# Causal masks written into the score banks by VectorE and ScalarE instead of by TensorE

## The chip, the core and the metric

The kernel runs on one core of a Trainium2 chip. The metric is the device time of the whole program in microseconds, as the median of several executions. A core has five engines with in-order queues of their own: TensorE (PE in the profile, with its weight loads as PEld), VectorE (DVE), ScalarE (ACT), GpSimd (POOL) and SyncE (SP). They wait for one another through semaphores only. TensorE writes its products to PSUM, which has eight banks of 128 partitions x 512 fp32 values, here named by their use.

## The reference, cut to what matters

Two decoder layers over x of shape (8, 128, 256): each has self attention, cross attention on a context of 64 columns, and an expert block; after each comes a residual sum and a layer norm. Three of the four attentions are causal:

```python
# layer 0 self attention (16 heads of 16)
scores = jnp.einsum('bqhd,bkhd->bhqk', Q, K)
scores = jnp.where(causal[None, None], scores, -jnp.inf)
attn = jax.nn.softmax(scores, axis=-1)
# layer 0 cross attention (32 heads of 8): no mask
# layer 1 self attention (32 heads of 8, rotary): causal
# layer 1 cross attention (16 heads of 16): causal as well
```

## The kernel before, in words

The four attentions run in one stage, the function `attention`, as a list of 32 units: 8 batch rows of ATTN0 (units 0 to 7), of CROSS0 (8 to 15), of ATTN1 (16 to 23) and of CROSS1 (24 to 31). ATTN0, ATTN1 and CROSS1 are causal. A unit has 2 pairs of banks of work if its heads are wide (ATTN0, CROSS1) and 4 if they are narrow (CROSS0, ATTN1), 96 pairs in all, 64 of them causal. The loop goes over places w and steps c of a place (2 or 4 steps). Between CROSS0 and ATTN1 four places host layer 0's expert block, whose products use the S^T banks and PV. All queues are written out by this one loop, so that the order on each engine is fixed by the code.

Softmax needs each row's maximum along q, and the sum with the values needs P transposed. So scores are made twice. S (queries on partitions) goes to two banks SB[0], SB[1], where VectorE takes maxima over each head (L730, in `maxima`). S^T (keys on partitions) goes to STB[0], STB[1]; small products (L356, `subtract_max`) take the maxima off, ScalarE takes exp into pt (L590, in `exponentials`), and `values` (L428) multiplies pt with the values into bank PV.

One step of TensorE is: `fill`, which writes the S pair of a later unit and the S^T pair of the present one together (L336 for S, L344 or L348 for S^T, L356 for the maxima), then `values` of the pair before, then other small jobs of neighbouring units. In a narrow place step c = 0 has the projection (L279), c = 1 the transposes of PV and of q and k (L437, L322) and then `values`, c = 2 the output projection (L447, L455, with ScalarE's copy atT, L608, between), c = 3 the transpose of the maxima (L407; copied back by ScalarE as nm, L602) and of x (L262). A wide place puts the same into two steps: c = 0 has the projections, `values`, the value projection (L302 or L304) and L437; c = 1 has `values`, L407, L262, L447 and L455.

VectorE's queue in a step begins with `maxima` and goes on with what the place needs: norm (L797), rope (L675 to L683), the query and key copies (L690, L707, L712, L699), `normalise` (L761, L768: reciprocal and att, for which `values` at c = 1 waits), `residual` (L782 to L791). ScalarE's begins with `exponentials` and goes on with copies out of PSUM: qT (L562), pvs (L596), vaug (L579), nm, xT (L549), atT.

In a causal unit, `fill` starts each bank with a mask product: an identity of bf16 times a 128 x 512 bf16 mask (0, or -1e30 where masked), with start=True (L372 for SB, L384 for STB). The scores are then added onto it. `fill` waits for max_done (bank SB read) before the S mask products, and for exp_done (STB read) before the S^T ones; at a unit's first S^T pair also for nm_copied.

Of the kernel before, what the change touches and what calls it, by code (L numbers as in the profile page):

```python
# [21 lines left out]
ACT = mybir.ActivationFunctionType  # L22
# [68 lines left out]
class Stage:  # L91
# [5 lines left out]
    def sem(self, name):  # L97
        self.sems.append(self.nc.alloc_semaphore(f"{self.prefix}_{name}"))
        return self.sems[-1]
# [10 lines left out]
def attention(nc, cfgs, T, F):  # L110

    V = B * len(cfgs)
    FFN_AT, FFN_HOSTS = 2 * B, B // 2
    STEPS = 11
    own = [cfgs[v // B] for v in range(V)]
    n = [cfg.pairs for cfg in own]
    before = [sum(n[:v]) for v in range(V + 1)]
# [18 lines left out]
    def emptied(t, q):  # L136
# [2 lines left out]
            return 2 * (q - 1)  # L139
        return 2 * (4 * t + q - 2)  # L140

    def tile_of(w, c):

        return 2 * (w - FFN_AT) + c // 2 if FFN_AT <= w < FFN_AT + FFN_HOSTS else None
# [12 lines left out]
    with Stage(nc, "at") as stage, ExitStack() as ctx:  # L157
        sem = stage.sem
# [12 lines left out]
        v_ones = sem("v_ones")  # L171
        s_done = sem("s_done")
        max_done = sem("max_done")
        nm_hi = sem("nm_hi")
        nm_split = sem("nm_split")
        nmt_done = sem("nmt_done")
# [2 lines left out]
        exp_done = sem("exp_done")  # L179
# [34 lines left out]
        SB, STB = T.SB, T.STB  # L214

        def s_pair(w, c):

            nxt, soon = unit(w + 1), unit(w + 2)
            if c == hosted(w) - 1 and has(soon):
                return soon, 0  # L220
            if has(nxt) and c + 1 < n[nxt]:
                return nxt, c + 1
            return None

        def t_pair(w, c):
            v = unit(w)
            return (v, c) if has(v) and c < n[v] else None
# [21 lines left out]
        def _(pe):  # L249
# [75 lines left out]
            def scores(v, c, u, r):  # L325

                j = 2 * (c % 2) + u
                rows = slice(32 * j, 32 * j + 32)
                first = r == 0 and not own[v].causal
                bank = SB[u][:, r * 256:(r + 1) * 256]  # L330
                if own[v].wide:
                    q, k = T.qT[v % 3][rows, r * 128:(r + 1) * 128], T.kk[v % 3][rows, r * 256:(r + 1) * 256]
                else:
                    g = 2 * (c // 2) + r
                    q, k = T.qT[v % 3][rows, g * 128:(g + 1) * 128], T.kk[v % 3][rows, 0:256]
                return pe.matmul(bank, q, k, start=first, stop=r == 1, skip_group_check=True)  # L336

            def scores_t(v, c, u, r, e):

                j = 2 * (c % 2) + u  # L340
                rows = slice(32 * j, 32 * j + 32)
                if own[v].wide:
                    at = 2 * r + e
                    pe.matmul(STB[u][:, at * 128:(at + 1) * 128], T.kk[v % 3][rows, at * 128:(at + 1) * 128],  # L344
                              T.qT[v % 3][rows, r * 128:(r + 1) * 128], start=(at == 0 and not own[v].causal), stop=False, skip_group_check=True)
                elif r == 0 and e == 0:
                    kind = c // 2
                    pe.matmul(STB[u][:, :], T.kk[v % 3][rows, kind * 128:(kind + 1) * 128], T.qT[v % 3][rows, :],  # L348
                              start=not own[v].causal, stop=False, skip_group_check=True)
# [9 lines left out]
            def fill(w, c):  # L359

                s, t = s_pair(w, c), t_pair(w, c)
                if s:
                    v, i = s
                    p = before[v] + i
                    if i == 0:
                        pe.wait_ge(q_ready, v + 1)
                        pe.wait_ge(k_ready, v + 1)
                    for u in range(2):
                        if p > 0:
                            pe.wait_ge(max_done, 2 * (p - 1) + u + 1)  # L370
                        if own[v].causal:
                            pe.matmul(SB[u][:, :], T.ident_bf[:], T.mask_qk[:], start=True, stop=False, skip_group_check=True)  # L372
                if t:
                    v, i = t
                    p = before[v] + i
                    if i == 0:
                        pe.wait_ge(nm_copied, v + 1)
                        if v == FFN_AT:
                            pe.wait_ge(added, B * E0)
                    for u in range(2):  # L380
                        if p > 0:
                            pe.wait_ge(exp_done, 2 * (p - 1) + u + 1)
                        if own[v].causal:
                            pe.matmul(STB[u][:, :], T.ident_bf[:], T.mask_kq[:], start=True, stop=False, skip_group_check=True)  # L384
                for r in range(2):
                    if s:
                        for u in range(2):
                            last = scores(*s, u, r)
                            if r == 1:
                                last.then_inc(s_done, 1)  # L390
                    if t:
                        for e in range(2):
                            for u in range(2):
                                scores_t(*t, u, r, e)
                if t:
                    for slot in range(4):
                        for u in range(2):
                            last = subtract_max(*t, u, slot)
                            if slot == 3:
                                last.then_inc(st_done, 1)  # L400
# [108 lines left out]

            for w, c, count in hosts:  # L510
                fill(w, c)
                if count == 2 and c == 0:
                    project(unit(w + 2))
# [30 lines left out]
        def _(act):  # L544
# [36 lines left out]
            def exponentials(pair):  # L581
                if not pair:
                    return
                v, c = pair
                t = before[v] + c
                if t >= 2:
                    act.wait_ge(pv_done, t - 1)
                for u in range(2):
                    act.wait_ge(st_done, 2 * t + u + 1)
                    act.activation(T.pt[2 * (t % 2) + u][:, :], STB[u][:, :], ACT.Exp, scale=own[v].scale).then_inc(exp_done, 1)  # L590

            def copy_pv(m):
                if not has(m):
# [69 lines left out]
        def _(dve):  # L663
# [59 lines left out]
            def maxima(pair):  # L723
                if not pair:
                    return
                v, c = pair
                for u in range(2):
                    dve.wait_ge(s_done, 2 * (before[v] + c) + u + 1)
                    at = 4 * (c // 2)
                    dve.tensor_reduce(T.nmf[v % 2][:, 2 * (c % 2) + u, at:at + 4], SB[u][:, :].rearrange("p (h k) -> p h k", h=4),  # L730
                                      AX.X, ALU.max, negate=True).then_inc(max_done, 1)

            def split_maxima(m):
                if not has(m):
# [1121 lines left out]
```

## Time and profile before

| | us |
|---|---|
| median of 3 runs (lowest, highest) | 892.03 (890.66, 892.32) |
| the profiled execution, its own time | 893.14 |
| its span, first to last instruction | 891.2 |

| engine | busy us | share of the span |
|---|---|---|
| PE | 741.9 | 83% |
| PEld | 457.1 | 51% |
| DVE | 473.9 | 53% |
| ACT | 294.9 | 33% |
| POOL | 209.2 | 23% |

The mean granted TensorE clock was 0.952. The attention stage runs from about 40 to 572 us, the expert block of layer 0 from about 250 to 343 us within it; the rest up to 891 us is the routing and the experts of layer 1. Shares of busy time average over these stages, and a busy TensorE in this view is not one at its peak, since the ends of pipelined matmuls are modelled. A timeline row gives the start, the duration, the engine, the line and the tiles of a run of like instructions, and in brackets how long the engine sat idle before it and what ended that.

### The profile page before, as it was taken

To read this page: it belongs to the slowest core of one execution; us is meant where nothing else is said; L and a number is where in the kernel's file an instruction comes from. 1 tells how busy PE (TensorE), PEld (TensorE's weight loads), DVE (VectorE), ACT (ScalarE), POOL (GpSimd) and SP (SyncE) were. 2 spreads that over 40 slices of the span, in tenths; PEclk is the share of its full clock that TensorE was granted. 3 is DMA by queue.
4 is the path that set the end of the run, shared out by engine and by line. 5 is a ranking of instruction groups with operands and counts; after the bars stand their busy time and mean duration, and the time that the engine had idled before them with its cause. 6 is when DMAs were issued, how large, how long until landed. Compare 5 with 4: busy or idle time off the path is not lost. (4 is left out here: it accounts for less than half of the span.)

```text
span 891.2 us, 18175 instructions
## 1 busy us (share of the span) xinstructions
PE 741.9 (83%) x6832; PEld 457.1 (51%) x6887; DVE 473.9 (53%) x1240; ACT 294.9 (33%) x702; POOL 209.2 (23%) x253
## 2 busy tenths in 40 slices
PE   3589987877799999999999998699699999999900
PEld 3457765555554455655566666467344433434400
DVE  5755565566448886455453454259533333333447
ACT  0013233444420102333333333233265544555400
POOL 3111222010000000000000000054456556665500
PEclk9999999999969999999999999879899999999955
DMA  9493002000000000000000000087122222222273
GB/s 295 122 293 110 2 3 95 1 3 1 2 1 1 0 1 1 1 1 2 2 1 2 1 3 1 1 224 214 32 75 84 78 84 80 82 84 78 73 244 103
DMA packets 48123, 55.28 MB, mean 62 GB/s; under 512 B 7366, under 2 KB 43174, under 8 KB 47334
## 3 DMA queue, kind: packets, MB, share of 16 engines
q1 hardware_dynamic: 38246, 34.11, 13.2%
q0 software_dynamic: 6656, 16.85, 5.6%
q10 hardware_dynamic: 3136, 3.15, 1.1%
q8 instruction: 58, 0.95, 0.5%
q14 instruction: 27, 0.22, 0.1%
HBM read 41.45 MB, written 12.65 MB: 61 GB/s over the span
## 5 line engine op out<-in xcount | busy, mean ns | idle before, releaser
L730 DVE TENSOR_REDUCE nmf<-bank 128x4 f32<-128x512 f32 x192 | 123.7, 686 | 123.6 <-PE bank L336 123.5
L590 ACT ACTIVATE pt<-bank 128x512 f32<-128x512 f32 x192 | 104.2, 595 | 252.8 <-PE bank L356 252.8
L336 PE MATMUL bank<-kk,qT 32*128 32x256 f32 x768 | 109.2, 401 | 15.9 <-ACT pt L590 8.3
L928 POOL TENSOR_TENSOR rstd<-vare,half 128x1 f32<-128x1 f32 x32 | 17.5, 546 | 376.9 <-DVE vare L791 376.9
L336 PEld LDWEIGHTS bank<-kk,qT 32*128 32x128 f32 x768 | 67.2, 184 | 51.2 <-issue 35.3
L1531 PE MATMUL bank<-wgu,g_xgT 128*64 x256 | 90.5, 476 | 2.1 <-ACT g_xgT L1568 1.2
L1531 PE MATMUL bank<-g_wgu,g_xgT 128*64 128x352 f32 x256 | 90.5, 476 | 0.0
L356 PE MATMUL bank<-nm,sel 32*128 32x128 f32 x768 | 84.5, 338 | 0.0
L1496 POOL DMA_INDIRECT out_rows<-g_og,g_out_row x64 | 63.9, 998 | 64.9 <-DVE g_og L1600 54.5
L348 PE MATMUL bank<-qT,kk 32*128 32x512 f32 x256 | 74.6, 659 | 2.0 <-ACT pt L590 1.5
L1551 PE MATMUL bank<-wd,g_hT 128*64 x256 | 68.9, 392 | 0.2
L1551 PE MATMUL bank<-g_wd,g_hT 128*64 128x256 f32 x256 | 69.0, 392 | 0.0
L1491 POOL DMA_INDIRECT g_xg<-x_rows,g_x_row x64 | 62.6, 978 | 23.0 <-issue 18.2
L356 PEld LDWEIGHTS bank<-nm,sel 32*128 32x128 f32 x768 | 57.4, 191 | 18.1 <-issue 18.1
L1600 DVE COPY g_og<-bank 128x256 f32<-128x256 f32 x64 | 27.0, 421 | 65.9 <-remote 52.6
L491 PE MATMUL bank<-f_m,f_xT 128*128 128x512 f32 x128 | 59.6, 605 | 0.6 <-DVE f_acc L837 0.5
L1582 ACT ACTIVATE g_wgu<-wgu 128x704 f32 x64 | 50.7, 792 | 14.5 <-issue 9.1
L428 PE MATMUL bank<-pt,vaug 128*32 128x128 f32 x1024 | 43.0, 287 | 10.3 <-DVE att L768 9.6
L1594 DVE TENSOR_TENSOR g_h<-bank,g_sil 128x176 f32<-128x176 f32 x64 | 21.7, 339 | 55.9 <-ACT g_sil L1572 43.6
L1531 PEld LDWEIGHTS bank<-wgu,g_xgT 128*64 128x64 f32 x256 | 30.1, 137 | 33.2 <-issue 31.3
L1551 PEld LDWEIGHTS bank<-wd,g_hT 128*64 128x64 f32 x256 | 29.8, 136 | 21.7 <-issue 12.5
L1568 ACT ACTIVATE g_xgT<-bank 128x256 f32<-128x256 f32 x64 | 24.1, 377 | 40.0 <-remote 29.4
(242 smaller groups left out, 1346.5 us busy)
## 6 DMA issues: line engine op xcount, KB each, us to landing
wgu<-in_L_ffn_w_gate SPq DMA_DIRECT2D x4, 1408.0 KB
wgu<-in_L_ffn_w_up SPq DMA_DIRECT2D x4, 1408.0 KB
wd<-in_L_ffn_w_down SPq DMA_DIRECT2D x32, 176.0 KB
g_y<-out_rows SPq DMA_DIRECT2D x4, 768.0 KB, 16.7
g_y<-out_rows ACTq DMA_DIRECT2D x4, 768.0 KB, 17.4
sparse_table<-f_m_re SPq DMA_DIRECT2D x2, 1024.0 KB
f_m_re<-sparse_table SPq DMA_DIRECT2D x2, 1024.0 KB, 5.9
f_idx_row<-in_L_ffn_mask_idx SPq DMA_DIRECT2D x1, 1024.0 KB
```

What stands on the lines that cost most here:

```text
L336: return pe.matmul(bank, q, k, start=first, stop=r == 1, skip_group_check=True)
L348: pe.matmul(STB[u][:, :], T.kk[v % 3][rows, kind * 128:(kind + 1) * 128], T.qT[v % 3][rows, :], start=not own[v].causal, stop=False, skip_ ...
L356: return pe.matmul(STB[u][:, slot * 128:(slot + 1) * 128], T.sel[rows, which, :], T.nm1[rows, :], start=False, stop=slot == 3, skip_group_ ...
L428: last = pe.matmul(PV[quarter * COL:(quarter + 1) * COL, at * 128:(at + 1) * 128], cfg.stationary(vaug(v), kv), T.pt[2 * (t % 2) + u][:, s ...
L491: last = pe.matmul(expert_bank(t, q)[:, :], F.xT[t % 2][:, j * 128:(j + 1) * 128], F.m[:, j, 2 * q:2 * q + 2, :], start=(j == 0), stop=(j ...
L590: act.activation(T.pt[2 * (t % 2) + u][:, :], STB[u][:, :], ACT.Exp, scale=own[v].scale).then_inc(exp_done, 1)
L730: dve.tensor_reduce(T.nmf[v % 2][:, 2 * (c % 2) + u, at:at + 4], SB[u][:, :].rearrange("p (h k) -> p h k", h=4), AX.X, ALU.max, negate=Tru ...
L1491: pool.indirect_dma_start(G.xg[n % 4][:], None, G.x_rows[:, :], bass.IndirectOffsetOnAxis(ap=G.x_row[:, n:n + 1], axis=0)).then_inc(gather ...
L1496: pool.indirect_dma_start(G.out_rows[:, :], bass.IndirectOffsetOnAxis(ap=G.out_row[:, n:n + 1], axis=0), G.og[n % 4][:], None).then_inc(sc ...
L1531: last = pe.matmul(gu[n % 2][rows, 0:2 * MI], G.xgT[n % 2][:, j * 128:(j + 1) * 128][:, rows], w, start=(j == 0), stop=(j == KT - 1), skip ...
L1551: last = pe.matmul(down_bank[n % 2][rows, 0:D], G.hT[n % 2][:, j * 128:(j + 1) * 128][:, rows], w, start=(j == 0), stop=(j == 1), skip_gro ...
L1582: act.activation(G.wgu[n % 2][:], T.wgu[:, bass.ds(unit, 1), :, :].rearrange("p a k n -> p (a k) n"), ACT.Copy).then_inc(wgu_ready, 1)
```

## The change

The masks are now in memory as before, but they are copied into the PSUM banks: VectorE copies mask_qk into SB[u] right behind the pair's two maxima, and ScalarE copies mask_kq into STB[u] right behind the pair's two exponentials. `fill` waits for these copies (s_masked, st_masked) where it waited for max_done and exp_done, and begins with the scores, added onto what lies in the bank. The very first pair has no pair before it, and the first S^T pair of ATTN1 follows the expert block in these banks; these keep mask products. 63 of 64 S pairs and 62 of 64 S^T pairs change over.

```diff
+    pair_units = [v for v in range(V) for _ in range(n[v])]
+    s_masks = [p for p in range(1, len(pair_units)) if own[pair_units[p]].causal]
+    st_masks = [p for p in s_masks if p != before[FFN_AT]]
...
                     for u in range(2):
-                        if p > 0:
+                        if p in s_masks:
+                            pe.wait_ge(s_masked, 2 * s_masks.index(p) + u + 1)
+                        elif p > 0:
                             pe.wait_ge(max_done, 2 * (p - 1) + u + 1)
-                        if own[v].causal:
+                        else:
                             pe.matmul(SB[u][:, :], T.ident_bf[:], T.mask_qk[:], start=True, stop=False, skip_group_check=True)
...
                     for u in range(2):
-                        if p > 0:
+                        if p in st_masks:
+                            pe.wait_ge(st_masked, 2 * st_masks.index(p) + u + 1)
+                        elif p > 0:
                             pe.wait_ge(exp_done, 2 * (p - 1) + u + 1)
-                        if own[v].causal:
+                        if own[v].causal and p not in st_masks:
                             pe.matmul(STB[u][:, :], T.ident_bf[:], T.mask_kq[:], start=True, stop=False, skip_group_check=True)
...
                     act.activation(T.pt[2 * (t % 2) + u][:, :], STB[u][:, :], ACT.Exp, scale=own[v].scale).then_inc(exp_done, 1)
+                if t + 1 in st_masks:
+                    for u in range(2):
+                        act.wait_ge(exp_done, 2 * t + u + 1)
+                        act.activation(STB[u][:, :], T.mask_kq[:], ACT.Copy).then_inc(st_masked, 1)
...
                                       AX.X, ALU.max, negate=True).then_inc(max_done, 1)
+                p = before[v] + c
+                if p + 1 in s_masks:
+                    for u in range(2):
+                        dve.wait_ge(max_done, 2 * p + u + 1)
+                        dve.tensor_copy(SB[u][:, :], T.mask_qk[:]).then_inc(s_masked, 1)
```

VectorE's queue in a place of ATTN1, steps c = 0 and c = 1, before (bank0 and bank1 are SB, bank4 is PV, bank5 and bank6 hold projections; line numbers are those of each kernel):

```order
L730 TENSOR_REDUCE nmf0_153<-bank0 128x4 [waits at_s_done]
L730 TENSOR_REDUCE nmf0_153<-bank1 128x4 [waits at_s_done]
L797 TENSOR_SCALAR x_all_51<-res_179,mv_65,rstd_62 128x256 [waits at_rstd_done]
L675 TENSOR_TENSOR rope_a_183<-bank5,rope_131 128x320 [waits m_cleared]
L678 TENSOR_TENSOR rope_b_184<-bank5,rope_131 128x40x4 x2
L683 TENSOR_TENSOR qs1_163<-rope_a_183,rope_b_184 128x20x16 [waits m_pe,m_act,at_rope_a]
L730 TENSOR_REDUCE nmf0_153<-bank0 128x4 [waits at_s_done]
L730 TENSOR_REDUCE nmf0_153<-bank1 128x4 [waits at_s_done]
L761 RECIPROCAL rec_178<-bank4 128x32 [waits at_pvt_done]
L768 TENSOR_TENSOR att_176<-bank4,rec_178 128x16x2x8 [waits at_at_done,at_rec_done]
```

The same place in the changed kernel, from the first of these steps up to att:

```order
L744 TENSOR_REDUCE nmf0_153<-bank1 128x4 [waits at_s_done]
L750 CAST bank0<-mask_qk_136 128x512 [waits at_max_done]
L750 CAST bank1<-mask_qk_136 128x512 [waits at_max_done]
L816 TENSOR_SCALAR x_all_51<-res_179,mv_65,rstd_62 128x256 [waits at_rstd_done]
L689 TENSOR_TENSOR rope_a_183<-bank5,rope_131 128x320 [waits m_cleared]
L692 TENSOR_TENSOR rope_b_184<-bank5,rope_131 128x40x4 x2
L697 TENSOR_TENSOR qs1_163<-rope_a_183,rope_b_184 128x20x16 [waits m_pe,m_act,at_rope_a]
L744 TENSOR_REDUCE nmf0_153<-bank0 128x4 [waits at_s_done]
L744 TENSOR_REDUCE nmf0_153<-bank1 128x4 [waits at_s_done]
L750 CAST bank0<-mask_qk_136 128x512 [waits at_max_done]
L750 CAST bank1<-mask_qk_136 128x512 [waits at_max_done]
L780 RECIPROCAL rec_178<-bank4 128x32 [waits at_pvt_done]
```

Two copies now stand between the maxima and rope, and two between the maxima and the reciprocal.

ScalarE's queue in a place of ATTN1, steps c = 2 and c = 3, before (bank2 and bank3 are STB, bank7 holds the transposed att):

```order
L590 ACTIVATE pt0_164<-bank2 128x512 [waits at_st_done,at_pv_done]
L590 ACTIVATE pt1_165<-bank3 128x512 [waits at_st_done]
L608 ACTIVATE atT_177<-bank7 128x256 [waits at_at_done]
L590 ACTIVATE pt2_166<-bank2 128x512 [waits at_st_done,at_pv_done]
L590 ACTIVATE pt3_167<-bank3 128x512 [waits at_st_done]
L602 ACTIVATE nm1_161<-bank6 128x128 [waits at_nmt_done]
L549 ACTIVATE xT_175<-bank5 128x256 [waits m_loaded]
```

and in the changed kernel:

```order
L600 ACTIVATE pt0_164<-bank2 128x512 [waits at_st_done,at_pv_done]
L600 ACTIVATE pt1_165<-bank3 128x512 [waits at_st_done]
L604 ACTIVATE bank2<-mask_kq_137 128x512 [waits at_exp_done]
L604 ACTIVATE bank3<-mask_kq_137 128x512 [waits at_exp_done]
L622 ACTIVATE atT_177<-bank7 128x256 [waits at_at_done]
L600 ACTIVATE pt2_166<-bank2 128x512 [waits at_st_done,at_pv_done]
L600 ACTIVATE pt3_167<-bank3 128x512 [waits at_st_done]
L604 ACTIVATE bank2<-mask_kq_137 128x512 [waits at_exp_done]
L604 ACTIVATE bank3<-mask_kq_137 128x512 [waits at_exp_done]
L616 ACTIVATE nm1_161<-bank6 128x128 [waits at_nmt_done]
L559 ACTIVATE xT_175<-bank5 128x256 [waits m_loaded]
```

Two copies now stand ahead of atT and two ahead of nm.

## Rows read from the trace of the kernel before

**Rows 1.** Windows: busy time by engine; one ATTN1 unit, then the expert block's end.

```profile
357.40:375.30 17.90, 16.39 (x184) 10.70 (x186) 8.75 (x19) 6.37 (x14) 0.00 (x0) 1.00 0.01 2
311.50:342.50 31.00, 30.18 (x118) 15.60 (x120) 26.04 (x77) 2.49 (x9) 1.08 (x2) 1.00 0.00 1
```

**Rows 2.** Groups by line and form: mask products; busy us, mean ns, idle before.

```profile
L384 PE MATMUL bank<-mask_kq,ident_bf 128*128 128x512 bf16 x112 | 34.7, 380 | 2.1 <-issue 0.9 <-ACT pt L590 0.7
L372 PE MATMUL bank<-mask_qk,ident_bf 128*128 128x512 bf16 x89 | 30.1, 380 | 3.8 <-DVE nmf L730 1.5 <-issue 0.3
```

**Rows 3.** Timeline, ATTN1, a step c = 1.

```profile
379.92 0.48 PE L336 MATMUL bank<-kk,qT 32*128 32x256 f32 x2
...
381.12 1.29 DVE L730 TENSOR_REDUCE nmf<-bank 128x4 f32<-128x512 f32 x2 [0.48 <-PE bank L336]
...
382.71 0.42 DVE L768 TENSOR_TENSOR att<-bank,rec 128x256 f32<-128x256 f32 x1
...
383.28 0.64 PE L428 MATMUL bank<-pt,vaug 128*32 128x128 f32 x16 [0.69 <-DVE att L768]
...
384.82 0.48 PE L336 MATMUL bank<-kk,qT 32*128 32x256 f32 x2
```

**Rows 4.** Timeline, ATTN1, the step c = 2 behind it.

```profile
386.45 1.09 ACT L590 ACTIVATE pt<-bank 128x512 f32<-128x512 f32 x2 [3.23 <-PE bank L356]
...
387.42 0.39 ACT L608 ACTIVATE atT<-bank 128x256 f32<-128x256 f32 x1
...
387.87 1.13 PE L455 MATMUL bank<-a_wo,atT 128*128 128x256 f32 x4 [0.56 <-ACT atT L608]
...
388.83 0.59 PE L372 MATMUL bank<-mask_qk,ident_bf 128*128 128x512 bf16 x2
...
389.79 0.48 PE L336 MATMUL bank<-kk,qT 32*128 32x256 f32 x2
```

**Rows 5.** Timeline, ATTN1, the steps c = 3 and c = 0.

```profile
392.39 0.28 ACT L602 ACTIVATE nm<-bank 128x128 fp32r<-128x128 f32 x1
...
393.26 0.48 PE L336 MATMUL bank<-kk,qT 32*128 32x256 f32 x2
...
397.07 0.49 DVE L675 TENSOR_TENSOR rope_a<-bank,rope 128x320 f32<-128x320 f32 x1 [1.00 <-PE bank L279]
...
397.83 0.48 PE L336 MATMUL bank<-kk,qT 32*128 32x256 f32 x2
...
398.06 0.49 DVE L683 TENSOR_TENSOR qs<-rope_a,rope_b 128x320 f32<-128x320 f32 x1
```

**Rows 6.** Timeline, CROSS0, without masks.

```profile
205.01 1.08 ACT L590 ACTIVATE pt<-bank 128x512 f32<-128x512 f32 x2 [1.83 <-PE bank L356]
...
206.24 0.48 PE L336 MATMUL bank<-kk,qT 32*128 32x256 f32 x2 [0.74 <-ACT pt L590]
```

**Rows 7.** Groups by line and form: copies of 512 columns and more.

```profile
L1606 DVE COPY g_wd<-wd 128x512 f32 x64 | 27.7, 432 | 17.5 <-issue 15.5 <-PE bank L1551 2.0
L596 ACT ACTIVATE pvs<-bank 128x512 f32<-128x512 f32 x32 | 19.3, 602 | 10.4 <-PE bank L428 10.4
L1582 ACT ACTIVATE g_wgu<-wgu 128x704 f32 x64 | 50.7, 792 | 14.5 <-issue 9.1 <-PEq L107 4.5
```

**Rows 8.** Timeline, wide places: ATTN0 c = 0, then CROSS1 c = 0.

```profile
95.06 0.42 DVE L690 TENSOR_TENSOR qT<-bank,b_q 128x256 f32<-128x256 f32 x1 [0.39 <-PE bank L289]
...
505.45 0.48 PE L336 MATMUL bank<-kk,qT 32*128 32x256 f32 x2
...
508.78 0.38 ACT L562 ACTIVATE qT<-bank 128x256 f32<-128x256 f32 x1 [0.59 <-PE bank L292]
...
508.78 0.69 DVE L712 TENSOR_TENSOR kk<-bank,kinds 128x512 f32<-128x512 f32 x1
...
509.38 0.60 ACT L596 ACTIVATE pvs<-bank 128x512 f32<-128x512 f32 x1 [0.22 <-PE bank L428]
...
511.55 0.48 PE L336 MATMUL bank<-kk,qT 32*128 32x256 f32 x2
```

More of the change, by code:

```diff
@@ L173, in attention @@
         max_done = sem("max_done")
+        s_masked = sem("s_masked")
+        st_masked = sem("st_masked")
         nm_hi = sem("nm_hi")
```

## The prediction, made before the changed kernel ran

> **What bounds the kernel now.** I read the page's 40 slices first, and then windows over the attention stage. TensorE leads in it: in one ATTN1 unit of 17.90 us it is busy for 16.39, VectorE for 8.75 and ScalarE for 6.37, at a granted clock of 1.00 [rows 1]. By these shares TensorE has the work and the other two have room, and the change would be a plain gain. The shares hide the order, though. I then read the groups of mask products [rows 2], and last the timeline of single steps, from one first score product (L336) to the next, because that is where a chain through ScalarE or VectorE shows.
>
> The steps repeat to 0.01 us, so one of each sort will do. In ATTN1 step c = 1 goes from 379.92 to 384.82, 4.90 us; in it TensorE sits idle for 0.69 until VectorE has made att (L768) [rows 3]. Step c = 2, from 384.82 to 389.79, is 4.97 us; TensorE idles 0.56 until ScalarE has made atT (L608), which runs right behind the two exponentials [rows 4]. Step c = 3 goes to 393.26, 3.47 us, and nm (L602, done at 392.67) stands close ahead of its end; step c = 0 goes to 397.83, 4.57 us [rows 5]. The four make the unit of 17.91 us. So the path runs from the scores through the maxima or the exponentials to a small copy behind them, and back to TensorE. The change puts its copies into exactly this gap.
>
> **What goes.** Four mask products stand ahead of a full causal fill. The first of the S ones starts at 388.83 and the first score product at 389.79: 0.96 us for four and the hand-over [rows 4]. A 380 ns row of them [rows 2] overlaps its neighbour, so its duration is not its price. From L455's start at 387.87 to the first mask product are 0.96 us too; without masks I keep 0.10 for the hand-over, so the fill gains 0.86, or 0.43 for two products. 63 + 62 pairs of products at 0.43 are 54 us if TensorE never waited, the ceiling of the gain.
>
> **What a copy costs.** The trace has no copy from SBUF into PSUM, on either engine. ScalarE copies 512 columns out of PSUM in 602 ns, and 704 columns from SBUF to SBUF in 792 [rows 7]; two exponentials of 512 take 1.09 together [rows 4], so each further one in a row adds about 0.50. I take 1.00 for the two copies; ends are 0.74 and 1.50 (37% per copy off or half on top). VectorE needs 0.69 for 512 columns out of PSUM [rows 8] and 1.29 for two maxima [rows 3], but only 432 ns for 512 columns of fp32 between SBUF tiles [rows 7]. I take 1.29 a pair, since one side is PSUM as in the maxima; ends are 0.80 and 1.50.
>
> Here rows at 0.69 and at 0.43 disagree, and which one counts decides part of the sum. The Trainium skill (VectorE: DVE Perf Modes, Why PSUM operands drop a tier) says that an operand in PSUM rules out the mode that uses both SBUF ports, and that fp32 is left at one element a cycle. By that rule the slow row is the right one; by the fast row the sum below is some 10 us less. The rows named show both speeds, though none with PSUM as destination.
>
> Waiting costs too: exponentials end at 206.09 and TensorE's next product starts at 206.24, 0.15 later [rows 6].
>
> **ATTN1, step by step,** times from the first score product of each step.
> - c = 0: maxima start at 1.21 as in c = 3's twin and end at 2.50, copies end at 3.79, the next fill can start at 3.95. TensorE itself would be there at 4.57 - 0.86 = 3.71. So 3.95, a gain of 0.62. But VectorE's norm (0.4) and rope are behind the copies. Rope took 397.07 to 398.55, 1.48 us [rows 5], and now ends at about 5.5.
> - c = 1: its maxima could start at 3.95 + 1.21 = 5.16 on that clock and start at 5.5, 0.33 late. They end at 1.54 + 1.29 = 2.83 of this step, the copies at 4.12, reciprocal and att 0.8 later at 4.92; `values` starts 0.15 after that, and the fill 0.58 behind it (1.54 before [rows 3], less four masks and hand-over, 0.96). 5.65 against 4.90: +0.75. Without rope it is 5.3.
> - c = 2: atT is 1.00 late, four masks are gone: 4.97 + 1.00 - 0.86 = 5.11, +0.14.
> - c = 3: nm is ready 2.88 into the step before, now at 3.88; the fill at about 4.10 against 3.47, +0.63. VectorE's copies end at 3.79 and are hidden.
>
> The sum is 18.8 against 17.91, +0.9 a unit. Six units with rope or its like: +5.4; the last two, without: +0.6.
>
> **Wide places.** In step c = 0 of ATTN0, the query copy L690 waited 0.39 for TensorE [rows 8]; 1.29 of copies leave it 0.90 late, and with it L302 and L437 and the fill, against 0.86 saved: +0.04. In c = 1 atT decides as above: +1.00 - 0.86 = +0.14. Five units: +1. In c = 0 of CROSS1 ScalarE's qT waited 0.59, and pvs behind it 0.22 more [rows 8], which takes up nearly all of its 1.00. VectorE's kk (0.69) comes 1.1 late and is ready at about 5.2 of a step that was 6.10, so just in time. The step gains 0.80, six times: -4.8; c = 1 loses 0.14 six times: +0.9.
>
> **Ends of the runs of causal units.** At the first three fills of ATTN0 no S^T work covers the copies: the fill came right behind the maxima, now behind 1.29 of copies; with two masks gone +0.9 each, and the first two c = 1 steps a little: +3. In the last four steps of ATTN0 and the last three of CROSS1 only S^T masks are left: a copy pair of 1.00 on ScalarE's chain against 0.43 saved, +0.57, seven times +4, of which I put 2 to ATTN0 (one step there has four masks) and 1.7 to CROSS1.
>
> **The expert block's end.** Five S pairs of ATTN1 are copied between 311 and 342, where VectorE is busy for 26.04 of 31.0 [rows 1]. 5 x 1.29 = 6.45 us are added. Part of the 4.96 idle are gaps between dependent instructions; I take 3 as usable: +3.5. ATTN1's first S^T pair waits for the last of VectorE's sums here, so this is on the path. GpSimd, SyncE and the DMA queues are neither moved nor waited on in another way.
>
> **Sum.** ATTN0 1 + 3 + 2 = 6; expert block 3.5; ATTN1 6; CROSS1 -4.8 + 0.9 + 1.7 = -2.2. Together +13.3. The profiled execution took 893.14 (span 891.2 and 1.9 around it), 1.1 above the median; 892.03 + 13.3 = 905.3. Some of the waits will overlap with others that I counted apart, so I forecast 904.
>
> **Rivals.**
> 1. Cheap copies, faster. If writing into PSUM costs ScalarE 0.37 a copy and VectorE 0.40, c = 2 is 4.97 + 0.74 - 0.86 = 4.85 and c = 3 about 3.8, c = 1 5.2, c = 0 3.7: 17.6 a unit, -2.4 in eight; ATTN0 0 to -1, the expert block +1.4, CROSS1 -4.6. Some -7, 885. It decides at 0.43 per ScalarE copy, where atT's delay equals the masks. For it: a destination no row has. Against: the shortest 512-column row on ScalarE is at 0.6.
> 2. VectorE at its fast row alone, ScalarE as taken. c = 1 is about 5.05 and the start of ATTN0 1.5 cheaper: ATTN1 +1.4, expert block +1.4, ATTN0 +1.5, CROSS1 -2.2: +2, 894. For it: the 432 ns row. Against: both its sides are SBUF.
> 3. Dear copies: ScalarE 1.50 a pair (a wait on its own semaphore that undoes the overlap, or a slower write). Each step of c = 1 wide, c = 2 and c = 3 adds 0.5, about 11 + 16 of them, with seven at the ends: +17 at most, of which VectorE's chain hides a third; 904 + 12 = 916.
> 4. All hidden: no copy is late anywhere, -54, 838. The idle of TensorE before L428 and L455 [rows 3, 4] speaks against it: both chains are late already.
>
> The clock is no rival of its own: TensorE had 1.00 here, and will be busy for less of the time; if stretches fell to the lower level, it would be on rival 3's side.
>
> **Chances.** Forecast (897 to 911) 0.62; rival 1 0.13; rival 2 0.11; rival 3 0.13; rival 4 0.01. A difference under 0.2% (1.8 us) can't be told from none here: rival 2 stands at its border and gives most of `same`. Faster 0.14, same 0.09, slower 0.77. Eight in ten lie in 892 to 916; the forecast's own range is 897 to 911.
>
> **What would show it.** Mask copies of about 0.6 us on ScalarE and 0.65 to 0.69 on VectorE; an ATTN1 unit of 18.8 us with steps of 3.95, 5.65, 5.1 and 4.1; CROSS1's c = 0 at 5.3; TensorE's waits on atT and att grown by about 1 us each, and new waits of the score products on the copies. It is wrong if L437 or the query copy in wide steps holds no longer, if copies take 0.4, or if the unit falls below 17.9.

## The result, and the profile after

The changed kernel takes 944.67 us, median of 4 runs (939.18 to 950.41), against 892.17 of the kernel before, measured beside it (890.66 to 892.63): ratio 1.0605, 95% interval 1.0559 to 1.0651. The forecast was 904, in a range of 897 to 911, with eight chances in ten for 892 to 916. The direction is right; the size is 52 us instead of 12. Here and below, the medians take in all executions, and the ratios leave out two in the chip's slower state (933.02 us of late and 1205.38 us of select).

The page of the kernel after: span, busy times, slices of TensorE and its granted clock, then costly groups (line, engine, tiles, shapes, count, busy us, mean ns, idle before them).

```profile
span 940.9 us, 18083 instructions
PE 748.5 (80%) x6637; PEld 478.1 (51%) x6637; DVE 548.2 (58%) x1366; ACT 361.2 (38%) x826; POOL 207.9 (22%) x253
...
PEclk9989798999969998778779899657979999999965
...
L342 PE MATMUL bank<-kk,qT 32*128 32x256 f32 x768 | 127.1, 453 | 37.8 <-ACT nm L616 15.3
...
L750 DVE CAST bank<-mask_qk 128x512 f32<-128x512 bf16 x126 | 80.4, 684 | 0.0
...
L604 ACT ACTIVATE bank<-mask_kq 128x512 f32<-128x512 bf16 x124 | 69.6, 606 | 0.0
...
L438 PE MATMUL bank<-pt,vaug 128*32 128x128 f32 x1024 | 47.3, 309 | 18.2 <-DVE att L787 18.2
```

The copies cost what was taken for them: 684 ns on VectorE, the speed of its row out of PSUM [rows 8]; 606 ns on ScalarE, where its row out of PSUM has 602 [rows 7]. What stands out is that TensorE has lost 250 mask products and is yet busier than before (748.5 against 741.9 us): the score products, the same 768 as before, take 453 ns instead of 401, `values` 309 instead of 287. Mean granted clock 0.883; it was 0.952.

The windows name the place. Columns: window, its length, busy us (count) of PE, PEld, DVE, ACT, POOL, granted clock, DMA share, GB/s. The first is ATTN1, from its first steady step to CROSS1's (before: 128.12 us, clock 1.00), the second the run of CROSS1's scores (69.66, 1.00), the third ATTN0's (93.29, 1.00).

```profile
373.70:525.24 151.54, 120.26 (x1218) 83.59 (x1219) 92.00 (x195) 74.82 (x163) 3.24 (x6) 0.81 0.00 1
525.24:594.62 69.38, 57.77 (x742) 45.62 (x742) 47.38 (x107) 37.53 (x90) 3.26 (x6) 0.94 0.01 2
46.56:152.71 106.15, 82.72 (x959) 67.54 (x958) 69.66 (x160) 41.00 (x90) 19.33 (x29) 0.89 0.29 81
```

ATTN1 alone is 23.4 us longer and ATTN0 12.9, and all three stages now have stretches at 1.2 GHz. Here is a stretch of ATTN1 that had the full clock, steps c = 3, 0 and 1 (timeline: start, duration, engine, line, tiles; in brackets the idle time before it and what ended it).

```profile
438.64 1.13 PE L465 MATMUL bank<-a_wo,atT 128*128 128x256 f32 x4 [1.59 <-ACT atT L622]
439.70 0.48 PE L342 MATMUL bank<-kk,qT 32*128 32x256 f32 x2
...
441.33 1.08 ACT L600 ACTIVATE pt<-bank 128x512 f32<-128x512 f32 x2 [2.74 <-PE bank L362]
...
442.11 1.27 DVE L750 CAST bank<-mask_qk 128x512 f32<-128x512 bf16 x2
442.30 1.12 ACT L604 ACTIVATE bank<-mask_kq 128x512 f32<-128x512 bf16 x2
...
443.33 0.28 ACT L616 ACTIVATE nm<-bank 128x128 fp32r<-128x128 f32 x1
...
443.82 0.48 PE L342 MATMUL bank<-kk,qT 32*128 32x256 f32 x2 [1.53 <-ACT nm L616]
...
447.68 0.48 PE L342 MATMUL bank<-kk,qT 32*128 32x256 f32 x2
...
449.13 1.28 DVE L744 TENSOR_REDUCE nmf<-bank 128x4 f32<-128x512 f32 x2
...
450.32 1.28 DVE L750 CAST bank<-mask_qk 128x512 f32<-128x512 bf16 x2
...
451.89 0.42 DVE L787 TENSOR_TENSOR att<-bank,rec 128x256 f32<-128x256 f32 x1
...
452.46 0.64 PE L438 MATMUL bank<-pt,vaug 128*32 128x128 f32 x16 [2.11 <-DVE att L787]
453.04 0.48 PE L342 MATMUL bank<-kk,qT 32*128 32x256 f32 x2
```

TensorE waits three times a unit: 1.59 for atT, 1.53 for nm, 2.11 for att, where before it waited 0.56 and 0.69 [rows 3, 4]. The waits are those that the prediction names. The steps are short all the same: 4.12, 3.86, 5.36 us. Two units earlier the same wait for att is followed by this (windows with the step c = 1's rest, then `values` and c = 2, c = 3, c = 0; columns as above):

```profile
404.34:409.12 4.78, 2.67 (x29) 2.15 (x30) 4.71 (x12) 3.09 (x7) 0.00 (x0) 1.00 0.00 0
409.12:417.33 8.21, 7.30 (x58) 4.48 (x58) 2.94 (x7) 2.39 (x5) 0.00 (x0) 0.51 0.01 2
417.33:422.55 5.22, 3.69 (x41) 2.53 (x40) 3.03 (x6) 2.49 (x6) 0.00 (x0) 0.78 0.01 3
422.55:429.10 6.55, 6.55 (x44) 4.58 (x45) 3.33 (x8) 2.67 (x6) 0.54 (x1) 0.54 0.00 1
```

In the windows the clock is at 1.00 up to the end of the wait and near 0.5 behind it, and the same work takes longer: the step c = 2 lasts 7.38 us instead of 5.13, c = 0 6.55 instead of 3.86. The products themselves show it (timeline of TensorE, a fill at the full clock and the next at the lower one):

```profile
404.34 0.48 PE L342 MATMUL bank<-kk,qT 32*128 32x256 f32 x2
404.36 0.70 PE L354 MATMUL bank<-qT,kk 32*128 32x512 f32 x2
...
409.12 0.90 PE L438 MATMUL bank<-pt,vaug 128*32 128x128 f32 x16 [2.11 <-DVE att L787]
409.95 0.80 PE L342 MATMUL bank<-kk,qT 32*128 32x256 f32 x2
409.97 1.22 PE L354 MATMUL bank<-qT,kk 32*128 32x512 f32 x2
```

The kernel before has TensorE waits too, but smaller (14 of 0.35 us or more in the whole ATTN1 window, 8.4 us in all, the longest 0.70; after 22, 31.4 and 2.11), and its three causal stages have 1.00 throughout. So two theories were set up for the 49.7 us of added span: A, the path of copies alone is worth about 15 and the rest is TensorE's clock, which falls because TensorE waits; B, the path is dearer than worked out, and the clock is a symptom that costs little.

### The profile page after: what moved, and what is told of

The parts are those of the page before. It is cut to its first block and busy times, and to the rows that moved or that the text cites. A ratio compares the mean times of both kernels' runs of the same rounds, so it can differ in the third digit from the quotient of the medians.

```text
span 940.9 us, 18083 instructions
## 1 busy us (share of the span) xinstructions
PE 748.5 (80%) x6637; PEld 478.1 (51%) x6637; DVE 548.2 (58%) x1366; ACT 361.2 (38%) x826; POOL 207.9 (22%) x253
## 5 line engine op out<-in xcount | busy, mean ns | idle before, releaser
L342 PE MATMUL bank<-kk,qT 32*128 32x256 f32 x768 | 127.1, 453 | 37.8 <-ACT nm L616 15.3
L342 PEld LDWEIGHTS bank<-kk,qT 32*128 32x128 f32 x768 | 77.7, 208 | 67.2 <-issue 30.3
L362 PE MATMUL bank<-nm,sel 32*128 32x128 f32 x768 | 97.1, 377 | 0.0
L354 PE MATMUL bank<-qT,kk 32*128 32x512 f32 x256 | 84.2, 738 | 2.1 <-ACT pt L600 1.5
L750 DVE CAST bank<-mask_qk 128x512 f32<-128x512 bf16 x126 | 80.4, 684 | 0.0
L362 PEld LDWEIGHTS bank<-nm,sel 32*128 32x128 f32 x768 | 67.3, 222 | 20.9 <-issue 20.9
L604 ACT ACTIVATE bank<-mask_kq 128x512 f32<-128x512 bf16 x124 | 69.6, 606 | 0.0
L438 PE MATMUL bank<-pt,vaug 128*32 128x128 f32 x1024 | 47.3, 309 | 18.2 <-DVE att L787 18.2
L350 PE MATMUL bank<-qT,kk 32*128 32x128 f32 x512 | 46.8, 334 | 0.0
```

The source lines that it names most:

```text
L362: return pe.matmul(STB[u][:, slot * 128:(slot + 1) * 128], T.sel[rows, which, :], T.nm1[rows, :], start=False, stop=slot == 3, skip_group_ ...
L604: act.activation(STB[u][:, :], T.mask_kq[:], ACT.Copy).then_inc(st_masked, 1)
L750: dve.tensor_copy(SB[u][:, :], T.mask_qk[:]).then_inc(s_masked, 1)
```

## The experiments

Nine further kernels. Ratios are to the kernel before, measured beside each on the same chip. The last two ran on another chip, where before took 901.29 us instead of 892, so that of these only ratios and stage times are compared. Stage times and clocks are those of one profiled execution; that of s_only is its fastest (909.88 us, 10 us below its median). In the expectations, A is the one that speaks of the clock, B the one of the path alone. Waits are those of TensorE of 0.35 us or more in the ATTN1 window: number, sum and longest in us.

| kernel | median us | ratio (95% interval) | ATTN1 us | ATTN1 clock | waits |
|---|---|---|---|---|---|
| after | 944.67 | 1.0605 (1.0559, 1.0651) | 151.5 | 0.81 | 22, 31.4, 2.1 |
| s_only | 920.3 | 1.0304 (1.0268, 1.0339) | 136.1 | 0.99 | 22, 24.8, 1.9 |
| t_only | 921.69 | 1.034 (1.0265, 1.0415) | 133.4 | 0.97 | 22, 22.8, 1.6 |
| no_masks | 849.34 | 0.9505 (0.946, 0.955) | 108.2 | 1.00 | 22, 13.9, 1.0 |
| both | 978.16 | 1.0945 (1.0906, 1.0984) | 163.5 | 0.92 | 22, 26.9, 1.9 |
| busy | 915.79 | 1.0267 (1.0217, 1.0318) | 133.2 | 1.00 | 6, 2.9, 0.6 |
| late | 926.37 | 1.0308 (1.0231, 1.0384) | 148.0 | 0.79 | 21, 25.9, 2.2 |
| select | 872.13 | 0.9757 (0.9698, 0.9816) | 115.5 | 1.00 | 15, 11.3, 1.9 |
| busy_c1 | 952.82 | 1.0582 (1.0515, 1.065) | 144.9 | 0.89 | 16, 23.7, 1.9 |
| busy_c3 | 948.59 | 1.0505 (1.0427, 1.0584) | 144.3 | 0.88 | 17, 23.9, 2.1 |

**s_only: only the S banks get copies.** The S^T masks stay products.

```diff
-    st_masks = [p for p in s_masks if p != before[FFN_AT]]
+    st_masks = []
...
-                        else:
+                        if own[v].causal and p not in s_masks:
                             pe.matmul(SB[u][:, :], T.ident_bf[:], T.mask_qk[:], start=True, ...)
```

> Only VectorE copies masks (63 S pairs); the S^T masks stay TensorE products. By the step model at a granted clock of 1.00: an ATTN1 unit of c = 0 4.4, c = 1 6.1, c = 2 4.5, c = 3 4.4, 19.5 us against 17.91; CROSS1 5.7 and 5.15; whole kernel about 905. Clock theory (TensorE's longer waits let the granted clock fall to its lower level in stretches, which is what made 944 out of 906): the wait in c = 1 is longer than in the changed kernel while c = 2 has its old 0.56, so stretches at 0.5 appear in ATTN1 and hardly any in CROSS1, and the kernel takes 915 to 935. Path-only rival (the extra 38 us are delays the steps do not explain): 905 with clock 0.95.

**t_only: only the S^T banks get copies.** The S masks stay products, by the same second edit as in s_only.

```diff
-    s_masks = [p for p in range(1, len(pair_units)) if own[pair_units[p]].causal]
-    st_masks = [p for p in s_masks if p != before[FFN_AT]]
+    causal = [p for p in range(1, len(pair_units)) if own[pair_units[p]].causal]
+    s_masks = []
+    st_masks = [p for p in causal if p != before[FFN_AT]]
```

> Only ScalarE copies masks (62 S^T pairs); the S masks stay TensorE products. By the step model at a clock of 1.00: ATTN1 c = 0 4.14, c = 1 4.47, c = 2 5.54, c = 3 4.1, 18.25 us a unit; CROSS1 5.67 and 6.14; whole kernel about 900. Clock theory: waits of up to 1.6 us before L455 and in c = 3, fewer than in the changed kernel, since c = 1 keeps its 0.69: some stretches at 0.5, 900 to 920, and less than s_only loses. Path-only rival: 900 with clock 0.95.

The windows over ATTN1, s_only and then t_only:

```profile
368.07:504.21 136.14, 111.27 (x1277) 72.37 (x1276) 92.44 (x195) 46.43 (x105) 3.24 (x6) 0.99 0.01 1
```
```profile
369.78:503.20 133.42, 110.49 (x1273) 73.30 (x1273) 62.01 (x143) 74.53 (x162) 3.34 (x7) 0.97 0.01 1
```

Each half alone keeps the clock near 1.00 in ATTN1 and costs 28 to 29 us in the whole. They don't add to after's 52: added up they would make 57. Nor is the clock untouched elsewhere: in ATTN0 it is 0.90 in both, and that stage takes 101.9 and 105.8 us against before's 93.3. What they add in ATTN1 is 8.0 and 5.3 us, together 13.3, while both together add 23.4: there the two halves do more harm than their sum. The steps are 4.31, 5.66, 4.53 and 4.31 us (c = 0 to 3) for s_only and 4.13, 4.48, 5.56 and 3.97 for t_only, 18.81 and 18.14 a unit. Both medians are near those expected by the clock (915 to 935; t_only 2 us above its 900 to 920), but mainly not through ATTN1, and that t_only would lose less than s_only is not met.

**no_masks: how much is the masks' own work, and does less work alone lower the clock?** The mask products go, and no copies come; this kernel leaves the causal mask out and attends to all keys. The edit, against before (S banks; the S^T banks alike):

```diff
-                first = r == 0 and not own[v].causal
+                first = r == 0
...
-                        if own[v].causal:
-                            pe.matmul(SB[u][:, :], T.ident_bf[:], T.mask_qk[:], start=True, ...)
```

> No masks anywhere: neither products nor copies (softmax over all keys). Nothing new is waited for; only TensorE's work of 54 us is gone. Step model at 1.00: ATTN1 3.7 + 3.9 + 4.1 + 3.1 = 14.9 us a unit, CROSS1 5.2 + 4.7, whole kernel about 843. If less work between unchanged waits is enough to let the clock fall, stretches at 0.5 appear in the causal attentions and the kernel takes 860 to 890. If it takes long waits, the clock stays 0.95 and the time is 843.

```profile
337.16:445.36 108.20, 94.68 (x1218) 68.20 (x1219) 61.12 (x142) 46.22 (x105) 3.25 (x6) 1.00 0.01 2
```

TensorE has the very products of after (1218 in the window) and the clock stays at 1.00. So the missing work alone does not lower it. The unit takes 15.1 us. The masks are worth 43 us of the kernel before, short of the 54 called the ceiling; in ATTN1 part of the difference is TensorE's waits, 13.9 us instead of 8.4. The median is 6 us above the 843 expected; the clock is at 1.00 in the windows of ATTN0 and CROSS1 too, so those 6 do not come from the clock there.

**both: copies made, and mask products too.** The products overwrite the copies (start=True); TensorE has all its work back, behind the waits for the copies.

```diff
-                        else:
+                        if own[v].causal:
                             pe.matmul(SB[u][:, :], T.ident_bf[:], T.mask_qk[:], start=True, ...)
...
-                        if own[v].causal and p not in st_masks:
+                        if own[v].causal:
                             pe.matmul(STB[u][:, :], T.ident_bf[:], T.mask_kq[:], start=True, ...)
```

> The copies of the changed kernel and, behind the waits for them, the mask products as before (start=True, so they overwrite what was copied). The path has both: ATTN1 4.9 + 6.5 + 6.0 + 5.1 = 22.4 us a unit at a clock of 1.00, whole kernel about 950. The waits are as long as in the changed kernel, with more work between them. If the length of the waits drops the clock, it falls here as well: over 980. If the share of time in which TensorE works does, it falls less than in the changed kernel: 950 to 970, mean clock over 0.90.

```profile
389.84:553.37 163.53, 134.98 (x1332) 82.27 (x1331) 92.61 (x195) 74.81 (x163) 3.24 (x6) 0.92 0.00 1
```

978 lies between the two forecasts (over 980 if the length of the waits decides, 950 to 970 if the share of TensorE's work does) and settles neither; the overall clock is 0.909, and 0.92 in ATTN1. With all of before's work the clock still falls, though less far than after's 0.81. That fits waits and work both bearing on it.

**busy: after's copies, and TensorE given something to do in the three waits.** Zero weights times a mask, added onto a bank, change no value. They are placed ahead of the product that waits: 9 before `values` at c = 1, 6 before `project_out`, 5 at the end of c = 3. Ahead of the 9 TensorE also waits until the bank that they go to has been read (res_done).

```diff
+            def busy(bank, count, m):
+                if not (has(m) and own[m].causal):
+                    return
+                for _ in range(count):
+                    pe.matmul(bank[:, :], T.zero_bf[:], T.mask_qk[:], start=False, stop=False, ...)
...
                     transpose_att(unit(w - 1))
+                    busy(PV, 6, unit(w))
                     project_out(unit(w - 1))
...
+                    if has(unit(w)) and has(unit(w - 1)):
+                        pe.wait_ge(res_done, max(1, unit(w - 1)))
+                        busy(M, 9, unit(w))
                     values(previous(w, c))
...
                     transpose_x(unit(w + 3))
+                    busy(PV, 5, unit(w))
```

> The changed kernel, with mask-sized products that change nothing (zero weights) laid on TensorE where it waits: in narrow places 9 into the output projection's bank at c = 1 ahead of the values, 6 into PV at c = 2 ahead of L465, 5 into PV at c = 3; in wide places 6 at c = 1 ahead of L465. Nothing is taken off any path, and TensorE has more to do. Clock theory: the granted clock in the causal attentions stays at 1.00, steps are 3.9, 5.4, 5.1 and 4.1 throughout, and the kernel is FASTER than the changed one, 900 to 912 against 944, though it does more. Path-only rival (the loss is made of waits): no faster than 944, or slower by what the products add.

Windows of ATTN1 and CROSS1, columns as before:

```profile
372.22:505.39 133.17, 126.54 (x1364) 82.11 (x1364) 91.80 (x195) 74.62 (x163) 3.24 (x6) 1.00 0.01 2
505.39:571.33 65.94, 62.01 (x778) 45.74 (x778) 47.15 (x107) 37.15 (x90) 3.25 (x6) 1.00 0.01 2
```

Groups of TensorE in ATTN1, first of after and then of busy (line, tiles, shapes, count, busy us, mean ns, idle before them):

```profile
L354 PE MATMUL bank<-qT,kk 32*128 32x512 f32 x116 | 42.2, 811 | 0.1
L342 PE MATMUL bank<-kk,qT 32*128 32x256 f32 x216 | 40.0, 499 | 10.4 <-ACT nm L616 8.1 <-ACT bank L604 1.9
```
```profile
L525 PE MATMUL bank<-mask_qk,zero_bf 128*128 128x512 bf16 x145 | 34.9, 379 | 0.0
L354 PE MATMUL bank<-qT,kk 32*128 32x512 f32 x116 | 32.7, 639 | 0.0
L342 PE MATMUL bank<-kk,qT 32*128 32x256 f32 x217 | 31.0, 398 | 4.4 <-ACT bank L617 3.9
```

This is the main result. Nothing was taken off the path; 145 products that do nothing were added, and ATTN1 is 18.4 us shorter (133.17 against 151.54), with the score products back at 639 and 398 ns. The whole kernel gains 29 us on after. B can't give that. It is also a reading of ATTN1's path without the clock: its steady steps take 3.86, 5.35, 5.13 and 4.12 us, as after's do where those have the full clock, so the fillers lengthen none, and its ATTN1 is 5.05 us longer than before's. The median lies 4 us above A's range. The fillers themselves are on the path at ATTN0's start, where there is no other work: its first three steps take 18.7 us at the full clock, against 14.4 in after and 11.2 in before. And busy still loses the clock once near ATTN1, at the expert block's end (0.70 from 350 to 360 us), where no filler was put. So the clock is worth more than the 29 us.

**late: the copies of S^T come behind atT.** In narrow c = 2 and wide c = 1 ScalarE copies the mask at the end of the step, so that atT is no longer held up.

```diff
                 exponentials(t_pair(w, c))
+                late = count == 4 and c == 2 or count == 2 and c == 1
+                if not late:
+                    copy_mask(t_pair(w, c))
...
+                if late:
+                    copy_mask(t_pair(w, c))
```

> The changed kernel with one move: at narrow c = 2 and wide c = 1 ScalarE copies the masks behind atT (and nm, xT) instead of ahead of them. Step model at 1.00: c = 2 4.2 instead of 5.1, CROSS1's c = 1 4.75 instead of 5.74, ATTN0's 4.75 instead of 5.6; whole kernel about 19 us under the changed one's path, 886, if the clock stayed. Clock theory: the long waits of c = 1 (narrow) and c = 3 are still there, those before L465 are back to 0.6; the clock falls less than in the changed kernel: 895 to 920. Path-only rival: 925 (944 less 19).

```profile
369.97:517.98 148.01, 121.96 (x1219) 85.18 (x1219) 92.26 (x195) 75.34 (x163) 3.25 (x6) 0.79 0.01 1
```

It gains 18 us on after by the medians, some 26 by the ratios. The median is at B's 925 and above A's 895 to 920; but B took after's loss as it stands, and the trace doesn't bear it out: the clock in ATTN1 is lower than ever. In the profiles 6.4 us of the gain are in CROSS1 (63.01 us against 69.38), 6.2 in ATTN0 (99.95 against 106.15, its c = 1 at 4.62 instead of 5.61), and only 3.5 in ATTN1, whose clock is 0.79. The step c = 2 is down to 4.14 us, the waits for atT are 0.6; those for att (2.2) and nm (1.5) are left, and they are enough. One long wait fewer a unit did not keep the clock up in ATTN1.

**select: copies only where they are hidden.** Two functions choose the pairs. On VectorE none in narrow c = 1 and 3, in the expert block's places, at the start, or in most wide c = 0; on ScalarE none in narrow c = 3 and in wide c = 0 without projection; the rest stay mask products, and ScalarE's copies come late as above. 33 S and 51 S^T pairs are copied.

```diff
+            if w < 0 or FFN_AT <= w < FFN_AT + FFN_HOSTS or not (has(unit(w)) and own[unit(w)].causal):
+                return None
+            if hosted(w) == 4 and c in (1, 3):
+                return None
+            if hosted(w) == 2 and c == 0 and (not has(unit(w + 2)) or own[unit(w + 2)] is not CROSS1):
+                return None
...
+            if hosted(w) == 4 and c == 3:
+                return None
+            if hosted(w) == 2 and c == 0 and not wide_host(unit(w + 2)):
+                return None
```

> Copies only where the step model hides them, products elsewhere. ScalarE copies in every causal step but narrow c = 3, and at narrow c = 2 and wide c = 1 behind atT; VectorE copies at narrow c = 0 and c = 2, at wide c = 1 and at CROSS1's c = 0, nowhere in the expert block or ahead of ATTN0's queries. Step model at a clock of 1.00: ATTN1 3.9, 4.9, 4.2, 3.5, 16.5 us a unit; CROSS1 5.3 and 4.75; ATTN0 6.0 and 4.75; whole kernel about 865. If less work on TensorE lets the clock fall as in the kernel without masks, 870 to 880; if the waits left let it fall as in the changed kernel, 890 or more.

```profile
356.94:472.44 115.50, 105.53 (x1262) 71.78 (x1262) 75.60 (x168) 66.45 (x147) 3.25 (x6) 1.00 0.01 2
472.44:532.41 59.97, 54.40 (x742) 42.57 (x742) 46.75 (x106) 36.81 (x88) 3.26 (x6) 1.00 0.01 2
```

It beats both kernels: ratio 0.9757 (0.9698 to 0.9816), a gain clear of noise, though whether it reaches 2% is not. The median is 7 us above the 865 expected. ATTN1's unit is 16.17 us (3.86, 4.70, 4.14, 3.47), and the clock stays at 1.00 there and in CROSS1; in ATTN0 it is 0.96.

**busy_c1 and busy_c3: which of the three waits is it?** As busy, but only the 9 products at c = 1, or only the 5 at c = 3. The wide places, and so ATTN0 and CROSS1, get no fillers in either.

```diff
-                    busy(PV, 6, unit(w))
...
-                    busy(PV, 5, unit(w))
```
```diff
-                    busy(PV, 6, unit(w))
...
-                        busy(M, 9, unit(w))
```

> Of the zero products only the 9 at narrow c = 1, ahead of the values, where TensorE waits 1.9 us for att. The waits of 1.6 before L465 (narrow c = 2, wide c = 1) and 1.5 in c = 3 are left open. If one long wait among short ones does no harm but several in a row do, as the kernel with S copies alone (1.9 us once a unit, clock 0.99) and the one with S^T copies alone (1.6 once a unit, 0.97) say, two neighbouring waits of 1.6 and 1.5 still cost: ATTN1's clock 0.85 to 0.95, kernel 925 to 938. If the longest wait of a unit decides, ATTN1 stays at 0.97 or more and the kernel takes 915 to 925.

> Of the zero products only the 5 at narrow c = 3. The waits of 1.9 (c = 1) and 1.6 (c = 2), which follow one another, are left open. If neighbouring waits count together, ATTN1's clock stays low, 0.80 to 0.92, and the kernel takes 928 to 942. If any break in the row is enough, 0.97 or more and 918 to 925.

What TensorE waited for in ATTN1 (sum us, times, longest us), busy_c1 and then busy_c3:

```profile
PE bank L465 <- ACT atT L632: 11.2, 7, 1.6
PE bank L342 <- ACT nm L626: 10.6, 8, 1.5
```
```profile
PE bank L438 <- DVE att L795: 12.6, 7, 2.1
PE bank L465 <- ACT atT L630: 9.9, 7, 1.6
```

By their ratios, on the first chip's 892 us, the two come to 944 and 937 us: busy_c1 lies above its 925 to 938, busy_c3 inside the 928 to 942 that it had if neighbouring waits count together, and both clocks (0.89, 0.88) are in the ranges given for that case. The other case of each, that filling one wait is enough, is not met. Filling one of the three waits gives back about a third of the 18.4 us in ATTN1 (6.6 and 7.2 us, the clock up from 0.81), and in the whole little: ratios 1.058 and 1.051 beside after's 1.061, in intervals that for busy_c1 overlap. Either way two waits of about 1.5 us or more a unit are left, as in late. Neither of these two alone is the culprit, nor by late the wait for atT.

## Why the prediction was wrong

**The cost of a copy, right to 0.1 us a pair.** 1.00 was taken for ScalarE's pair, and it takes 1.12; 1.29 for VectorE's, and 1.28 it is. The Trainium skill (VectorE: DVE Perf Modes, Why PSUM operands drop a tier) says that an operand in PSUM leaves fp32 at one element a cycle; the trace agrees as far as it can: with PSUM as destination VectorE takes 684 ns, the 0.69 us of its slow row [rows 8] and not the 432 ns of the fast one [rows 7]. Rivals 1 and 2 fall with it. Rival 3's price of 1.50 a pair is not seen either.

**The unit of ATTN1, right to 0.3 us a unit.** At the full clock the steps are 3.86, 5.35, 5.13 and 4.12 us against 3.95, 5.65, 5.1 and 4.1: 18.5 instead of 18.8. In c = 1 the copies end at 3.92 of the step, not 4.12, and reciprocal and att take 0.7 behind them, not 0.8: that is the 0.3. The term of +6 for eight units is +5.05 in the ATTN1 window, and some 1.1 more in the three steps ahead of it (busy against before). A slip in the sum did no harm: by the prediction's own steps the last two units, without rope, lose 0.55 each, 1.1 and not 0.6.

**CROSS1, right.** 5.32 for c = 0 and 5.74 for c = 1 against 5.3 and 5.7. At full clock its window is 65.9 us (busy) against 69.7: -3.7, and -3.9 was worked out for c = 0 and c = 1. In after 3.4 of that are lost to the clock.

**ATTN0, right in its steady steps.** c = 0 takes 6.46 and c = 1 5.61 at the full clock, against 6.43 and 5.45 in before: +0.19 a unit, where 0.18 was worked out. The rest of the 12.9 us lies at the start (the first six steps 31.0 us against 27.4), at the last four (23.2 against 18.4) and in steps between at the lower clock (one c = 0 takes 8.72). The lower clock is in the first two as well, so the path's share is only an estimate, 5 to 9 us for the 6 taken.

**The end of the expert block, right once its clock is taken out.** From ATTN1's first S scores to its first steady step after takes 48.92 us and busy 48.60, before 42.41: 6.5 and 6.2 more, where 3.5 was taken. About 1.1 of it lies in the last three steps, which are the first unit's own. The rest is in the block, and there a long wait comes first. Windows from the first S scores to the first S^T fill, then TensorE at the last S fill, before and after:

```profile
311.56:342.97 31.41, 30.59 (x120) 15.65 (x121) 26.34 (x77) 2.43 (x9) 1.08 (x2) 1.00 0.00 1
324.78:361.65 36.87, 31.94 (x112) 16.42 (x111) 32.41 (x88) 2.81 (x9) 1.08 (x2) 0.91 0.00 0
```
```profile
336.25 1.13 PE L336 MATMUL bank<-kk,qT 32*128 32x256 f32 x8
337.70 3.60 PE L491 MATMUL bank<-f_m,f_xT 128*128 128x512 f32 x8
```
```profile
351.61 2.08 PE L342 MATMUL bank<-kk,qT 32*128 32x256 f32 x8 [3.09 <-DVE bank L750]
354.32 5.51 PE L501 MATMUL bank<-f_m,f_xT 128*128 128x512 f32 x8
```

TensorE waits 3.09 us for VectorE's copy, and its next products come at the lower clock: from the fill's start to the end of the expert products 8.22 us instead of 5.05, 3.2 more (2.8 in busy). That leaves about 2.3 us of path in the block, or 3.4 with the three steps. VectorE's idle time there falls from 5.07 to 4.46 us although 3.2 us of lower clock are in the window; without them, by this estimate, some 1.3 would be left, so it used three or more of its five idle us, as the prediction supposed.

**The sum of the path, right.** 5 to 9 for ATTN0, 3.4, 5.05 and -3.7, with 1.5 behind CROSS1's last S scores (busy against before; the causal steps there add 6.7, partly at the lower clock, and the stretch behind the last output projection is 5.3 shorter, of which the cause is open): 11 to 15 against 13.3. Among the rivals, the "some -7" of rival 1 adds up to -6 from its own terms; nothing hangs on it.

**The step that failed** is the sentence "The clock is no rival of its own: TensorE had 1.00 here, and will be busy for less of the time; if stretches fell to the lower level, it would be on rival 3's side." It is the wrong way round. That TensorE would wait three times a unit instead of twice, and each time for 1.5 to 2.1 us instead of 0.6, is in the prediction's own steps; what was left out is that a TensorE that waits more can lose its clock, after which its own products stand on the path. The runs showed the price. By busy against after it is 18.4 us in ATTN1, 3.4 in CROSS1 and 5.3 behind it (the last causal steps take 6.3 to 7.5 us in after, 5.0 to 6.3 in busy). By windows and rows alone, as an estimate, it is 4 to 8 in ATTN0 and 3 at the expert block's end. So the clock is some 34 to 38 of the 49.7 us of added span; 29 of them are shown by a run. In the trace as a whole TensorE had the lower level for some 220 us (940.9 x (1 - 0.883) x 2), and in before for some 86 (891.2 x 0.048 x 2).

What stays open is which pattern of waits makes the clock fall. In ATTN1 it stayed up with shorter waits (no_masks, select: all but one of 1.0 or less; clock 1.00), and nearly with one long wait a unit beside shorter ones (s_only, t_only: 0.99 and 0.97); with two or three long ones it fell (after, late, busy_c1, busy_c3: 0.79 to 0.89). But s_only has nearly the sum of waits that late has (24.8 and 25.9 us), and `both` has less loss than after with waits nearly as long, so neither the sum nor the longest orders the runs. Nor need the long waits be those of neighbouring steps, as busy_c1 and busy_c3 might suggest: in late there is a step without one between them. That the products between the waits count too would fit, but isn't shown. The loss is also not the same in each unit: in late the clock is 1.00 from 406 to 436 us, one unit and a half with the same waits, and 0.50 from 495 to 514.

## What to carry to other kernels

Work taken from a busy TensorE and put on a chain for which TensorE waits costs twice: once on the chain, and once more if TensorE's clock falls with its new waits. So where the steps of a forecast lengthen TensorE's waits, put a case with the lower clock beside the sum, priced from rows at the lower level (here a step took 1.4 to 1.7 times as long: 7.38 for 5.13 us, 6.55 for 3.86), and read the granted clock by stage before anything else in the profile after. And choose the places: the same copies at the steps where the receiving engine's chain ends early gained 2.4%, where copies at all steps lost 6%.

## What the runs showed of the hardware beside

- Products with zero weights keep TensorE's clock at its upper level here: 145 of them in ATTN1 (busy) took it from 0.81 to 1.00, and made the stage 18.4 us shorter.
- ScalarE writes 512 columns from SBUF into PSUM in 606 ns (bf16 to fp32), about the 602 ns of its copy out of PSUM; VectorE needs 684 ns into PSUM and 0.69 us out of it.
- The granted clock moves between executions of one kernel, and the time does not follow it closely: after's four have 0.874 to 0.888, and the slowest (950.41 us) has the highest clock. Spreads of some 11 us are seen with and without long waits: after's runs cover 939 to 950 us, and ten runs of before 885 to 896.
